# A graph layer and an expert layer on one core: weight sums made one half step a sort group, the bias copied by GpSimd, a quarter of x fetched later, and two stages put in one block

## The reference

```python
def rgcn(x):                                   # x is the layer-normed input
    out = x @ root + bias
    for r in range(8):
        mask = (edge_type == r)
        sums = segment_sum(x[src] * mask[:, None], dst)
        cnt = segment_sum(mask, dst)
        out += (sums / maximum(cnt, 1)[:, None]) @ weight[r]
    return out

u = rgcn(norm(x)); z = concat([u, norm(x)]) @ w_gate + b_gate
x = x + tanh(u) * z + norm(x) * (1 - z)
x = x + grouped_swiglu_top2(norm(x))           # eight experts, two per token
```

## Time and profile before

| what | value |
|---|---|
| runs | 1873.48 us median of 3 (1866.82 to 1873.74) |
| the profiled execution | 1871.54 us, span 1869.8 us |
| TensorE, matmuls | 1716.4 us busy, 92% of the span, 7873 |
| TensorE, weight loads | 1407.0 us, 75% |
| VectorE | 1156.0 us, 62% |
| ScalarE | 613.3 us, 33% |
| GpSimd | 758.7 us, 41% |
| granted TensorE clock, mean | 0.965 |
| HBM | 245.90 MB read, 102.15 MB written, 186 GB/s |

### The profile page before, as it was taken

One profiled execution on the slowest core, in us unless ns is written; L12 is line 12 of the kernel. 1 busy time (PEld: TensorE's weight loads), 2 busy tenths in 40 slices (PEclk: granted clock), 3 DMA queues, 4 the chain that ended last, 5 costly groups with the idle time before them and its releaser, 6 DMA issues. The chain is left out here.

```text
span 1869.8 us, 21835 instructions
## 1 busy us (share of the span) xinstructions
PE 1716.4 (92%) x7873; PEld 1407.0 (75%) x7873; DVE 1156.0 (62%) x1492; ACT 613.3 (33%) x894; POOL 758.7 (41%) x663
## 2 busy tenths in 40 slices
PE   7999888999999999999699999989889967999993
PEld 6888677788888888888577777777668855787882
DVE  8557787864464342434389999988789876424200
ACT  3211111111231312122156565555432213545451
POOL 1013444105775565101156554554255524645531
PEclk9999999999999999999899999999989978999997
DMA  5247676322223434346688888878654445877645
GB/s 200 91 146 249 228 234 216 126 79 69 91 96 125 143 122 145 121 146 226 205 279 275 283 273 287 279 257 275 231 196 169 158 155 172 220 216 190 159 81 153
DMA packets 142344, 344.40 MB, mean 184 GB/s; under 512 B 19476, under 2 KB 35908, under 8 KB 142160
## 3 DMA queue, kind: packets, MB, share of 16 engines
q0 software_dynamic: 52112, 164.00, 29.1%
q1 hardware_dynamic: 90128, 179.00, 28.3%
HBM read 245.90 MB, written 102.15 MB: 186 GB/s over the span
## 5 line engine op out<-in xcount | busy, mean ns | idle before, releaser
L1080 POOL DMA_INDIRECT gathered<-Y,edge_row x184 | 217.4, 1182 | 234.6 <-PE banks L1197 188.4
L1099 ACT ACTIVATE ghi<-gathered,edge_w 128x1024 fp32r<-128x1024 f32 x184 | 211.4, 1152 | 174.3 <-DMA gathered<-Y,edge_row 159.1
L861 POOL DMA_INDIRECT edge_w<-INV,edge_key x184 | 210.6, 1145 | 130.9 <-DMA edge_w<-INV,edge_key 102.5
L1137 DVE SCALAR_TENSOR_TENSOR glo<-gathered,edge_w,ghi 128x1024 fp32r<-128x1024 f32 x184 | 232.3, 1281 | 46.9 <-ACT ghi L1099 46.2
L884 PE MATMUL banks<-whi,xhi 128*128 128x512 f32 x640 | 253.7, 396 | 0.6 <-DVE xlo L652 0.6
L885 PE MATMUL banks<-wlo,xhi 128*128 128x512 f32 x640 | 250.2, 391 | 0.0
L886 PE MATMUL banks<-whi,xlo 128*128 128x512 f32 x640 | 250.0, 391 | 0.0
L431 ACT ACTIVATE y_out<-banks 128x512 f32<-128x512 f32 x80 | 47.7, 597 | 385.7 <-PE banks L886 385.7
L1196 PE MATMUL banks<-ghi,sel 128*128 128x512 f32 x368 | 147.7, 401 | 21.5 <-DVE glo L1137 21.2
L1197 PE MATMUL banks<-glo,sel 128*128 128x512 f32 x368 | 144.6, 393 | 0.0
L884 PEld LDWEIGHTS banks<-whi,xhi 128*128 128x128 f32 x640 | 121.2, 189 | 25.5 <-DVE xlo L652 1.2
(11 more groups left out here) (315 smaller groups left out, 3600.9 us busy)
## 6 DMA issues: line engine op xcount, KB each, us to landing
raw<-in_L_ffn_w SPq DMA_DIRECT2D x24, 1024.0 KB, 10.3
Y<-y_out SPq DMA_DIRECT2D x80, 256.0 KB, 3.2
t_set<-in_L_gnn_weight POOLq DMA_DIRECT2D x64, 256.0 KB, 3.6
TW<-t_set POOLq DMA_DIRECT2D x64, 256.0 KB, 5.6
raw_chunk<-TW SPq DMA_DIRECT2D x64, 256.0 KB, 2.8
w_stage<-in_L_gnn_weight SPq DMA_DIRECT2D x30, 512.0 KB, 4.8
raw_chunk<-in_L_gnn_weight SPq DMA_DIRECT2D x48, 256.0 KB, 3.0
Y<-half_v SPq DMA_DIRECT2D x40, 256.0 KB, 2.3
```

The lines of the kernel that those rows point to most:

```text
L861: nc.gpsimd.indirect_dma_start(out=edge_w[:, t:t + 1], out_offset=None, in_=INV, in_offset=bass.IndirectOffsetOnAxis(ap=edge_key[:, t:t + ...
L1080: nc.gpsimd.indirect_dma_start(out=gath[t % GR][:], out_offset=None, in_=Y, in_offset=bass.IndirectOffsetOnAxis(ap=edge_row[:, t:t + 1], a ...
L1099: nc.scalar.activation(ghi[:, t % HR], gath[t % GR][:], ACT.Copy, scale=edge_w[:, t:t + 1]).then_inc(g_hi, 1)
L1137: v.scalar_tensor_tensor(glo[t % GR][:], gath[t % GR][:], edge_w[:, t:t + 1], ghi[:, t % HR].bitcast(F32), ALU.mult, ALU.subtract).then_in ...
```

## The change

1. `t_make` takes one half step. One is made after each of the 24 sort groups, the last eight beside relation 3, two behind each `split_lo(3, 1, q)`. `t_load(m + 2)` follows `t_store(m)`. `INV` is stored by GpSimd before half step 24 is stored, and the gathers of `edge_w` begin after half step 31. The values of the sort stay with VectorE.
2. The bias is loaded once by DMA and copied nine times by GpSimd: four copies after unit 23, five after unit 25.
3. The quarter of x comes back at the end of the first block's stores instead of before unit 25.
4. The two blocks become one. The waits of the border become waits of single engines: GpSimd waits for all stores of Y before its first gather, TensorE waits for its bank and for each quarter of the root weight. `steps()` begins the edge tiles later: the offset `LEAD` is 16, which puts the first behind chunk 17, so behind eighteen chunks.

The functions of the second block (`split_hi3`, `evacuate3`, `edges_hi`, `places`, `edges_lo`, `accumulate`, `edges`) move with it and are otherwise as they were, but for the lines shown.

```diff
--- before.py
+++ after.py
             sem("onehots_ready"), sem("onehots_used"), sem("place_onehots_ready"), sem("place_values_ready"))
         acc_set, inv_ready, inv_out, key_ready = (
-            sem("acc_set"), sem("inv_ready"), sem("inv_stored"), sem("keys_ready"))
+            sem("acc_set"), sem("inv_ready"), sem("inv_stored_then_bias_loaded"), sem("keys_ready"))
...
+        LAG_SPLIT, LAG_OUT, LEAD = 3, 4, 2 * KC
...
+                if (c + 1 - LEAD) * ET // (4 * half - LEAD) > t:
+                    yield "edges", t
+                    t += 1
...
                 for n in range(SN):
                     ahead = [c for c in range(KH * (n + 2) - 1, KH * (n + 3) - 1) if KH * 3 - 1 <= c < KH * SN]
-                    if n == SN - 3:
-                        sp.wait_ge(tile_done, TR * (SN - 3))
-                        for a, part in enumerate((xhi, xlo)):
-                            sp.dma_start(quarter(part, 1, 0).bitcast(F32),
-                                         X21[a].rearrange("p (k n) -> p k n", n=HN)).then_inc(x21_moved, 16)
                     for i in range(TR):
                         if i < len(ahead):
                             load_raw(ahead[i])
                         if n == SN - 1 and i in (1, 2):
                             load(R0, 0, i + 1)
-                for i in range(YB):
-                    sp.wait_ge(y_out[i], 16 * (R0 * 2 * NT // YB))
-                for i in range(TR):
-                    sp.wait_ge(row_moved[i], OUTS * (R - R0))
+                for a, part in enumerate((xhi, xlo)):
+                    sp.dma_start(quarter(part, 1, 0).bitcast(F32),
+                                 X21[a].rearrange("p (k n) -> p k n", n=HN)).then_inc(x21_moved, 16)
+                def load3(g, q):
+                    n = 4 * (g - 1) + q
+                    if n < 2:
+                        sp.wait_ge(w_lo, R0 * 8 + 4)
+                    if n >= 2:
+                        sp.wait_ge(w_lo3, n - 1)
+                    w = root if g < 2 else w_gate[D:2 * D, :]
+                    sp.dma_start(stage[:, q % 2], w_rows(w, q, g % 2)).then_inc(w_in3[q % 2], 16)
...
+                        sp.wait_ge(y_evac3, g * NT + j + 1)
+                        sp.dma_start(YX[g // 2, j * P:(j + 1) * P, (g % 2) * HALF:(g % 2 + 1) * HALF],
+                                     yout[:, j % 2]).then_inc(y_out3[j % 2], 16)
...
+                def evacuate3(g, j):
+                    act.wait_ge(y_ready3, g * NT + j + 1)
+                    if g * NT + j < 2:
+                        act.wait_ge(row_moved[j], OUTS * (R - R0))
+                    else:
+                        act.wait_ge(y_out3[j % 2], 16 * (g * (NT // 2) + j // 2))
+                    nc.scalar.activation(yout[:, j % 2], psum[j % 2][:], ACT.Copy).then_inc(y_evac3, 1)
-                def t_make(*steps):
-                    sets = [[t_set[:, m % TS, a, b] for a in range(2) for b in range(2)] for m in steps]
-                    for m, (b11, b12, b21, b22) in zip(steps, sets):
-                        dve.wait_ge(t_moved[m % TS], 64 * (m // TS) + 32)
-                        v.tensor_tensor(b22, b22, b12, ALU.subtract).then_inc(t_made, 1)
-                        v.tensor_tensor(b12, b12, b11, ALU.subtract).then_inc(t_made, 1)
-                    at = 4 * steps[0]
-                    for m, (b11, b12, b21, b22) in zip(steps, sets):
-                        dve.wait_ge(t_made, at + 2 * (m - steps[0]) + 1)
-                        v.tensor_tensor(b11, b22, b11, ALU.add).then_inc(t_made, 1)
-                    for m, (b11, b12, b21, b22) in zip(steps, sets):
-                        dve.wait_ge(t_made, at + 2 * len(steps) + m - steps[0] + 1)
-                        v.tensor_tensor(b21, b21, b11, ALU.subtract).then_inc(t_made, 1)
+                def t_make(m):
+                    b11, b12, b21, b22 = (t_set[:, m % TS, a, b] for a in range(2) for b in range(2))
+                    dve.wait_ge(t_moved[m % TS], 64 * (m // TS) + 32)
+                    v.tensor_tensor(b22, b22, b12, ALU.subtract).then_inc(t_made, 1)
+                    v.tensor_tensor(b12, b12, b11, ALU.subtract).then_inc(t_made, 1)
+                    dve.wait_ge(t_made, 4 * m + 2)
+                    v.tensor_tensor(b11, b22, b11, ALU.add).then_inc(t_made, 1)
+                    dve.wait_ge(t_made, 4 * m + 3)
+                    v.tensor_tensor(b21, b21, b11, ALU.subtract).then_inc(t_made, 1)
...
                             if sorts:
                                 g = (r - 1) * SG1 + h * SG1 // 2 + part
                                 columns(r, h * SG1 // 2 + part, g == 0)
-                                if 2 * g < T_STEPS:
-                                    t_make(2 * g, 2 * g + 1)
+                                t_make(g)
                             if part in SPLIT_PARTS and not (start and h == 0):
                                 split_lo(*((r, 1) if h == 0 else (r + 1, 0)), SPLIT_PARTS.index(part))
                 relation(0, False, start=True)
@@ -730,6 +829,9 @@
                 for r in range(1 + SORT_R, R0):
                     for q in range(4):
                         split_lo(r, 1, q)
+                        if r == R0 - 1:
+                            for m in (T_SORT + 2 * q, T_SORT + 2 * q + 1):
+                                t_make(m)
                     if r < R0 - 1:
                         for q in range(4):
                             split_lo(r + 1, 0, q)
...
+                dve.wait_ge(acc_set, NT - 1)
+                for i in range(2, 4):
+                    dve.wait_ge(row_moved[i], OUTS * (R - R0))
+                places(0)
+                places(1)
...
                     s, k, part = m // 8, m // 2 % KH, m % 2
-                    pool.wait_ge(t_made, 4 * (m // 2) * 2 + 8)
+                    pool.wait_ge(t_made, 4 * m + 4)
                     for a in range(2):
                         at = s * D + a * HALF + k * P
                         pool.dma_start(TW[at:at + P, :].rearrange("p (b n) -> p b n", b=2)
                                        [:, :, part * TQ:(part + 1) * TQ], t_set[:, m % TS, a]).then_inc(t_moved[m % TS], 16)
                 pool.wait_ge(hot_ready, 1)
-                for m in range(TS):
-                    t_load(m)
+                t_load(0)
+                t_load(1)
                 for m in range(T_STEPS):
+                    if m == SORT_R * SG1:
+                        pool.wait_ge(inv_ready, 1)
+                        pool.dma_start(INV.rearrange("(a b) c -> a (b c)", b=BT), inv[:]).then_inc(inv_out, 16)
                     t_store(m)
-                    if m % 2:
-                        for ahead in range(m + TS - 1, min(m + TS + 1, T_STEPS)):
-                            t_load(ahead)
-                pool.wait_ge(inv_ready, 1)
-                pool.dma_start(INV.rearrange("(a b) c -> a (b c)", b=BT), inv[:]).then_inc(inv_out, 16)
+                    if m + 2 < T_STEPS:
+                        t_load(m + 2)
                 pool.wait_ge(inv_out, 16)
                 pool.wait_ge(key_ready, 1)
                 for t in range(ET):
@@ -863,10 +1016,28 @@
                         in_offset=bass.IndirectOffsetOnAxis(ap=edge_key[:, t:t + 1], axis=0)).then_inc(w_gathered[t % 2], 16)
                 for i in range(2):
                     pool.wait_ge(w_gathered[i], 16 * ET // 2)
-                for j in range(NT):
-                    if j % TR == 0:
-                        pool.wait_ge(tile_done, TR * (SN - 4 if j == 0 else SN - 2))
-                    pool.dma_start(acc[:, j * D:(j + 1) * D], bias.partition_broadcast(P)).then_inc(acc_set, 16)
+                pool.wait_ge(tile_done, TR * (SN - 4))
+                pool.dma_start(acc[:, 0:D], bias.partition_broadcast(P)).then_inc(inv_out, 16)
+                pool.wait_ge(inv_out, 32)
+                for j in range(1, NT):
+                    if j == TR:
+                        pool.wait_ge(tile_done, TR * (SN - 2))
+                    nc.gpsimd.tensor_copy(acc[:, j * D:(j + 1) * D], acc[:, 0:D]).then_inc(acc_set, 1)
+                for i in range(YB):
+                    pool.wait_ge(y_out[i], 16 * (R0 * 2 * NT // YB))
+                for i in range(TR):
+                    pool.wait_ge(row_moved[i], OUTS * (R - R0))
+                pool.wait_ge(hy_out[0], 16 * 3 * (R - R0))
+                pool.wait_ge(hy_out[1], 16 * 2 * (R - R0))
+                pool.wait_ge(tile_done, TR * SN)
+                for t in range(ET):
+                    if t >= GR:
+                        pool.wait_ge(g_used, t - GR + 1)
+                    nc.gpsimd.indirect_dma_start(
+                        out=gath[t % GR][:], out_offset=None, in_=Y,
+                        in_offset=bass.IndirectOffsetOnAxis(ap=edge_row[:, t:t + 1], axis=0)).then_inc(g_in[t % GR], 16)
...
-        LAG_SPLIT, LAG_OUT = 3, 4
...
-                if (c + 1 - KC) * ET // (4 * half - KC) > t:
-                    yield "edges", t
```

(15 more changed lines are left out.)

257 lines of the change are left out of this document (114 added, 143 removed).

## The result

| | before | after |
|---|---|---|
| median | 1872.91 us of 4 (1866.82 to 1873.74) | 1840.67 us of 4 (1837.91 to 1841.78) |
| ratio, 95% interval | 1 | 0.9833 (0.9809 to 0.9857) |
| the profiled execution | 1871.54 us, span 1869.8 | 1841.78 us, span 1840.0 |
| end of unit 27 | 909.26 | 880.06 |
| first edge tile | 933.5 | 902.0 |

The account below looks back on a forecast made before the run. TensorE was taken to bound the kernel, waiting for VectorE in the sort, with the edge stage near three limits. Sort 29 plus border 4, 33 us off 1871.5, gave 1838.5, stated as 1839 us; range 1829 to 1850.

Parts of the forecast that it names:

- The sort: Sort groups: TensorE stops waiting for VectorE, intervals fall from 11.87 to 10.39 or 11.07 us; 29 us gained, bounds 21 and 31.
- (b): Rival, sort: only part comes back, as loads or chained operations are late; 1853 us, from 1849 to 1862; chance 0.07.
- (c): Rival, sort: VectorE waits for DMA traffic itself, mean interval stays 11.87 us, time within 9 us of 1871; chance 0.03.
- (d): Rival, sort: late loads stretch VectorE's group beyond 12.3 us, making the kernel slower, 1881 us or more; chance 0.02.
- The eight moved half steps: Beside relation 3: 14 us more VectorE work, covered by the first ring chunk's 11.72 us wait, 1 or 2 left; cost zero.
- the loads that go away return nothing either: Bias: dropping nine of ten loads gains zero, since TensorE was never short between 855 and 909 us.
- the 5.6 forecast: Border: TensorE's wait for the last quarter of the root weight, 5.6 us, takes the place of the border's wait.
- at most 0.7: Border: the first gathers, needing the stores of 921.17 landed, start at most 0.7 us earlier than before.
- The border: Between unit 27 and the edge tiles: +4 us gained, between bounds of +7.9 and -8.6, taken as nearer to TensorE's pace.
- rival (a): Border: the fetch of x collides with the first gathers, border gives 0 to -8.6 us, 1842 to 1851 us; chance 0.15.
- The clock: Border: TensorE runs about 4.7 us at 1.2 GHz instead of 2.4 behind the idle time that stays, costing 2.3 us.
- Eight chunks of lead: Border: edge tiles begin behind eighteen chunks instead of ten, putting TensorE 5.4 us ahead at the first edge tile.

Follow-up runs that it names:

- sort_only: The kernel before with part 1 of the change alone (one half step a sort group, loads two ahead): 1841.14 us, ratio 0.9849.
- load_one_ahead: The changed kernel with each half step's load issued one step ahead of its use instead of two: 1844.49 us, ratio 0.9898.
- bias_and_x_as_before: The changed kernel with ten bias broadcasts and the fetch of x before unit 25, both as in the kernel before: 1837.87 us, ratio 0.9827.
- x_early: The changed kernel with the quarter of x fetched before unit 25, as in the kernel before: 1835.67 us, ratio 0.9816.
- lead8: The changed kernel with edge tiles begun behind ten chunks (offset 8), as in the kernel before: 1842.98 us, ratio 0.9847.
- x_later: The changed kernel with the quarter of x fetched behind the second store of the new product, some 15 us later: 1836.42 us, ratio 0.9831.

## Why the prediction was right

**The sort was right in mechanism and in size.** 29 us were taken, 29.2 measured; VectorE's group fits because its four chained operations take the 1.7 us that were counted, and the wait for loads is gone. Rivals (b), (c) and (d) fell with the intervals, none of which is late, and `sort_only` has the gain without the rest.

**The eight moved half steps cost nothing, as said.** Their cover has another size than the step had it. The sums for the scheme wait for the last stores and start at 439.30; the first ring chunk then waits 3.71 us where it waited 11.72, so that 3.7 us of this cover are left and not 1 or 2. From VectorE's timeline of the changed kernel:

```profile
451.56 0.72 DVE L815 TENSOR_TENSOR ring_lo<-raw_chunk,ring_hi 128x512 fp32r<-128x512 f32 x1 [3.71 <-issue]
```

`load_one_ahead` spent it and found the rest behind it.

**The bias: the copies are covered, and "the loads that go away return nothing either" was the step that failed.** GpSimd's timeline has both blocks of copies:

```profile
830.38 4.45 POOL L1025 COPY acc<-acc 128x1024 f32<-128x1024 f32 x4 [3.53 <-DMA acc<-in_L_gnn_bias]
...
852.93 5.90 POOL L1025 COPY acc<-acc 128x1024 f32<-128x1024 f32 x5 [18.09 <-PE banks L1159]
```

That is 1.1 to 1.2 us a copy; the bounds of 0.5 and 3.3 held it, and the row of a two-input operation would have been three times too dear. Three ring splits beside them took 0.89 to 1.2 us where 0.69 is the rule, but over the whole kernel the splits are 77.9 us against 76.7 before, 1.2 us in all; `bias_and_x_as_before`, without copies, has 76.7 again. This agrees with the Trainium skill (SBUF — State Buffer, "Who interferes with whom") in kind: a VectorE instruction with two SBUF inputs does suffer beside a GpSimd instruction that reads SBUF. It was right not to take off the 3 us that the rule gave with copies of 3.3 us, since the copies are short and the splits have slack. What the ten broadcasts had cost was something else. The step asked only whether TensorE was short while they ran, and it was not; the last weight chunk was late by 7.4 us, and with it SyncE's loads of the root weight. Without the broadcasts the root quarters go out 5.1 us sooner (`x_early` against `bias_and_x_as_before`), so the wait for the last quarter is 3.1 us and not the 5.6 forecast, and the gathers start 4.2 us earlier and not "at most 0.7". (That wait stands before the fourth pair of chunks, as the working of the border has it; the list of signs, with "the third chunk pair", had slipped by one.)

**The border: +4 was forecast, 2 or 3 came, out of other terms, and luck held the sum together.** By the ratios of `sort_only` and of the changed kernel and its repeat it is 2 or 3 us, inside their intervals; by the trace the first edge tile is 2.3 us earlier, where the step had 1.4. Those 1.4 came as 1.6, the time by which TensorE had been later than the first low part (933.46 against 930.52 + 1.28), and 0.7 or so are what the next two terms leave. Two of the signs that the prediction had listed for being wrong did come: the edge tiles wait 28.9 us in the first profile (23.2 in the repeat), where more than 25 was the sign, and the very first of them waits 4.66 us for its row, as rival (a) has it. The terms of the border were:

- *The gathers start 4.2 us earlier*, because the bias is no longer broadcast. This is missing in the sum.
- *The fetch of x takes 3.4 to 3.8 us back* at the first row. This is rival (a)'s mechanism. It was priced between 0 and 9.3 us, and it came at well under half: the first row took 7.7 us instead of 4.3. The Trainium skill (DMA: Bandwidth & Descriptors, "Queues, rings and completion order") has each DMA engine take turns between queues. The trace agrees only from 895.6 us on, where the two queues move 0.67 and 0.73 MB side by side. In the 4 us before, the queue of the gathers moved nothing while the fetch's moved 1.62 MB, so the gathers did stand behind a part of it, and 2.5 us of the loss come from this. In the repeat the first row has landed at 899.7 us and the fetch only at 904.3, so the row doesn't wait for the whole fetch; why the gathers begin so late is open. The rival had its outcome (1842 or more) wrong, since it didn't know of the 4.2 us on the other side.
- *The clock* behind the idle time that stays was to cost 2.3 us. It cost about 1.6: eight matmuls from 888.1 us at a pitch of 0.43 us instead of 0.227, clock 0.87 in the window from 880 us. It isn't on the path, since TensorE waits for the first tile anyway.
- *Eight chunks of lead, counted as 5.4 us ahead, are worth 1 to 3 us* by `lead8`, which can't tell this from nothing. This is the step that matters most for how one thinks of the stage. It read "DMA share 86%, TensorE 95%: nearer to TensorE, so I take +4". In this stage TensorE's work doesn't set the time: 73 us less of it changed nothing that was measured. The edge tiles come when their rows and VectorE's parts come, and in all the kernels that leave no work out the stage takes its 406 to 416 us from the first tile on, whether that comes at +12.1 or at +24.8. So an earlier first tile is what was seen to pay.

The sum of the border held by luck: the fetch and the missing credit for the broadcasts, both about 4 us, cancel, and the lead that was overpriced had been cut down by the choice between the bounds. The forecast as a whole held because the 29 us of the sort, which were understood, make up nine tenths of it.

## What to carry to other kernels

In this stage, where TensorE, VectorE and the transfers are all near their limit, work done ahead by TensorE bought next to nothing; what paid was to start the first round earlier. So look at what stands before the first gather of such a stage: the last store it waits for, what is queued ahead of that store, and every large transfer that goes out beside it. To find out who sets the pace of a stage, take work out, of each engine alone and of both together, and look how often a buffer of the ring is waited for; busy shares of 90% don't tell.

## What the runs showed of the hardware

- Five broadcasts of a 4 KB row to 128 partitions, 0.5 MB each, on GpSimd's queue delay a 256 KB load that SyncE issues 2.8 us after them: it is used 10.2 us after its issue (856.5 to 866.72) and not 2.9 (`bias_and_x_as_before` against `x_early`). The root quarters, which wait for this chunk's split, went out 5.1 us later, while TensorE was not short.
- A gather that is issued 2.8 us behind a 2.6 MB fetch moves its first packet 4.2 us after its issue (changed kernel and repeat), without the fetch 1.7 us after it (`x_early`, `x_later`). From then on both queues move.
- GpSimd copies 128x1024 f32 in 1.1 to 1.2 us, a third of its 3.3 us for a two-input operation of this size.
- 73 us less matmul work in a stage in which TensorE was busy 93% left its length as it was (407.1 us, in the scatter of 406.6 to 414.6).
- The edge stage of one kernel took 414.6 us in one profile and 406.6 in another, while everything up to its first tile was the same to half a us.
- With five gather buffers a round takes 11.4 us in the changed kernel, of which 6.1 are from the issue of the gather to the start of its use; 161 of the 175 gathers between 900 and 1300 us wait for a buffer that TensorE hasn't freed.
